# A Fourier layer's forward transform with the x table as the stationary operand, and its output turned by eight transposes

## The reference, cut to what matters

```
x_ft = rfft2(h)                                   # only 12 x 12 low modes of two corners are used
out_ft[:, :, :12, :12]  = einsum('bixy,ioxy->boxy', x_ft[:, :, :12, :12],  w1)
out_ft[:, :, -12:, :12] = einsum('bixy,ioxy->boxy', x_ft[:, :, -12:, :12], w2)
h = irfft2(out_ft) + conv_1x1(h)                  # 32 channels
h = layer_norm(h)                                 # over channels
h = gelu(h)                                       # not after the last layer
```

## Time and profile before

| | before |
|---|---|
| median of 3 runs | 7909.72 us (7907.23 to 7939.83) |
| profiled execution: its time, its span | 7906.27 us, 7904.4 us |
| PE busy / PEld busy | 86% / 58% |
| DVE, ACT, POOL busy | 62%, 64%, 54% |
| granted TensorE clock, mean | 0.922 of 2.4 GHz |
| DMA | 835 MB, 106 GB/s over the span |

### The profile page before, as it was taken

One profiled execution on the slowest core, in us unless ns is written; L12 is line 12 of the kernel. 1 busy time (PEld: TensorE's weight loads), 2 busy tenths in 40 slices (PEclk: granted clock), 3 DMA queues, 4 the chain that ended last, 5 costly groups with the idle time before them and its releaser, 6 DMA issues. The chain is left out here.

```text
span 7904.4 us, 141712 instructions
## 1 busy us (share of the span) xinstructions
PE 6788.2 (86%) x45682; PEld 4620.4 (58%) x45682; DVE 4865.3 (62%) x7585; ACT 5032.1 (64%) x8721; POOL 4262.9 (54%) x1540
## 2 busy tenths in 40 slices
PE   7888789999799999799998899999999477777777
PEld 4555577777677777577776544444444255444555
DVE  7888657777467777477776333333333566777774
ACT  7888567778477777477777477777777233333332
POOL 7888457777267777177776144444444433333330
PEclk9999899999899999899999999999999687788888
DMA  2222344444444444444444411111111322333330
GB/s 84 94 98 94 129 157 158 159 158 155 162 144 159 154 156 156 153 155 158 152 159 138 140 50 45 49 50 44 50 47 41 99 67 68 69 69 69 69 68 3
DMA packets 597044, 835.29 MB, mean 106 GB/s; under 512 B 451944, under 2 KB 493032, under 8 KB 531304
## 3 DMA queue, kind: packets, MB, share of 16 engines
q1 hardware_dynamic: 596968, 834.27, 33.9%
HBM read 477.54 MB, written 356.58 MB: 106 GB/s over the span
## 5 line engine op out<-in xcount | busy, mean ns | idle before, releaser
L859 POOL TENSOR_TENSOR sb_rstd<-sb_var,sb_minus_half 128x16 f32<-128x16 f32 x1280 | 3690.0, 2900 | 2440.3 <-DVE sb_var L591 1219.3
L598 DVE TENSOR_TENSOR sb_unit<-H,sb_rstd 128x512 f32<-128x512 f32 x768 | 527.3, 687 | 517.1 <-POOL sb_rstd L859 511.7
L555 ACT ACTIVATE sb_pix<-sb_unit 128x512 f32<-128x512 f32 x768 | 827.7, 1078 | 0.0
L505 PEld LDWEIGHTS M<-sb_table,sb_pix 128*128 128x128 f32 x6144 | 712.1, 194 | 144.3 <-ACT sb_pix L555 125.1
L478 PE MATMUL H<-sb_conv_block,sb_act_in 128*128 128x128 f32 x6144 | 777.7, 280 | 0.0
L551 ACT ACTIVATE sb_act_px<-sb_unit 128x512 f32<-128x512 f32 x768 | 485.9, 633 | 451.0 <-DVE sb_unit L604 450.9
L478 PEld LDWEIGHTS H<-sb_conv_block,sb_act_in 128*128 128x128 f32 x6144 | 724.3, 194 | 38.2 <-issue 23.9
L505 PE MATMUL M<-sb_table,sb_pix 128*128 128x52 f32 x6144 | 737.0, 279 | 0.0
L591 DVE TENSOR_REDUCE sb_var<-sb_square 128x16 f32<-128x528 f32 x768 | 502.5, 696 | 236.4 <-ACT sb_square L544 236.4
L822 DVE COPY sb_act_out<-TC 128x512 f32<-128x512 f32 x256 | 177.0, 691 | 644.3 <-PE TC L672 644.3
L1812 ACT ACTIVATE blk_silu<-bank 114x260 f32<-114x260 f32 x384 | 148.7, 387 | 638.4 <-PE bank L1598 635.8
(11 more groups left out here) (273 smaller groups left out, 13588.2 us busy)
## 6 DMA issues: line engine op xcount, KB each, us to landing
act_scratch<-sb_act_out SPq DMA_DIRECT2D x256, 1024.0 KB, 3.9
sb_act_in<-act_scratch SPq DMA_DIRECT2D x256, 1024.0 KB, 5.3
spectrum_in<-sb_f_sb SPq DMA_DIRECT2D x512, 78.0 KB, 1.8
sb_x_in<-spectrum_in SPq DMA_DIRECT2D x48, 832.0 KB, 4.3
spectrum_out<-sb_y_sb SPq DMA_DIRECT2D x48, 832.0 KB, 4.6
sb_z_in<-spectrum_out SPq DMA_DIRECT2D x512, 78.0 KB, 5.1
blk_rows_b<-scan_rows SPq DMA_DIRECT2D x128, 260.0 KB, 7.2
blk_rows_bb<-scan_rows SPq DMA_DIRECT2D x128, 260.0 KB, 8.2
```

Source lines behind the costliest of these rows:

```text
L505: mm = e.matmul(M[u][:, 52 * g:52 * g + 52], pix[1 - p][:, at:at + 128], const("f1"), start=True, stop=True)
L555: e.activation(dst, unit[k % 2][:, :].rearrange("p (x c) -> p c x", c=16), gelu).then_inc(pix_ready, 1)
L598: e.tensor_tensor(rows, H[k][:, :].rearrange("p (y c) -> p y c", c=C), rstd[k][:, :].unsqueeze(2).to_broadcast([128, 16, C]), ALU.mult).th ...
L859: e.tensor_tensor(rstd[j][:, :], var[j][:, :], minus_half[:, :], ALU.pow).then_inc(rstd_ready, 1)
```

## The change

forward_x no longer has the pixels as the stationary operand but the x table (52 columns), and the pixels of act_px as the moving one. It runs once for each chunk, right after to_channels, with two products of 256 columns: channels 0 to 15 go to partitions 0 to 51 of bank TP, channels 16 to 31 to partitions 64 to 115. So pix and its second gelu (or copy) are gone, and 16 products a pair become 8. Their output has the frequencies on the partitions; ACT copies TP to a new buffer `spread` after every two chunks (`gather`), and `turn` transposes spread by eight transposes into M[0] and M[1], from which ACT fills f1_sb as before (`frequencies`). forward_y writes M[1] in place of TP, and the copy to f2_sb moves from DVE to ACT (`spectrum`). In the first pass DVE's last step of the norm writes act_px itself, so that ACT's copy into act_px is gone too. The channels come in another order, which the tables "f2" and "combine" take up. The order of the three engines' programs is written anew.

```diff
@@ forward_x, the same in pe_first and pe_mid (before: 16 products of 52 columns)
-                e.wait_ge(pix_ready, g0)
-                for u in range(2):
-                    for g in range(8):
-                        at = 128 * (8 * u + g)
-                        mm = e.matmul(M[u][:, 52 * g:52 * g + 52], pix[1 - p][:, at:at + 128], const("f1"),
-                                      start=True, stop=True)
-                    mm.then_inc(f1_done, 1)
+                if k == 0:
+                    at_least(e, gathered, 2 * pr)
+                elif k == 2:
+                    e.wait_ge(gathered, 2 * pr + 1)
+                at = 16 * (k % 2)
+                src = act_px[k % 2][:, :].rearrange("p (y c) -> p y c", c=C)
+                for h in range(2):
+                    dst = TP[64 * h:64 * h + 52, :].rearrange("p (c y) -> p y c", y=32)[:, at:at + 16, :]
+                    mm = e.matmul(dst, const("f1"), src[:, :, 16 * h:16 * h + 16], start=True, stop=True,
+                                  skip_group_check=True)
+                mm.then_inc(fx_done, 1)
+            def turn(pr):
+                e.wait_ge(gathered, 2 * pr + 2)
+                for u in range(2):
+                    for b in range(4):
+                        at = 128 * (4 * u + b)
+                        mm = e.transpose(M[u][:, 128 * b:128 * b + 116], spread[0:116, at:at + 128],
+                                         const("ident")[0:116, 0:116])
+                    mm.then_inc(f1_done, 1)
@@ forward_y
-                    mm = e.matmul(TP[64 * i:64 * i + 48, 0:16 * T26], const("f2"), src, start=True, stop=True,
+                    mm = e.matmul(M[1][64 * i:64 * i + 48, 0:16 * T26], const("f2"), src, start=True, stop=True,
@@ act_mid
-                dst = pix[q][:, :].rearrange("p (c x) -> p c x", c=16)[:, :, 32 * k:32 * k + 32]
-                e.activation(dst, unit[k % 2][:, :].rearrange("p (x c) -> p c x", c=16), gelu).then_inc(pix_ready, 1)
+            def gather(half, pr):
+                e.wait_ge(fx_done, 4 * pr + 2 * half + 2)
+                at_least(e, f1_done, 2 * pr)
+                e.activation(spread[0:116, :].rearrange("p (c y) -> p c y", c=16)[:, :, 32 * half:32 * half + 32],
+                             TP[0:116, :].rearrange("p (c y) -> p c y", c=16), ACT.Copy).then_inc(gathered, 1)
+            def spectrum(q, pr, stored):
+                e.wait_ge(f2_done, pr + 1)
+                at_least(e, st_x[q], stored)
+                e.activation(f2_sb[q][:, :], M[1][0:112, 0:16 * T26], ACT.Copy).then_inc(f2_ready, 1)
@@ dve_first, normal
+                at_least(e, fx_done, c - 1)
+                e.tensor_tensor(act_px[k % 2][:, :].rearrange("p (y c) -> p y c", c=C), rows,
+                                shift_row[:, :].unsqueeze(1).to_broadcast([128, 16, C]), ALU.add).then_inc(px_ready, 1)
```

More of the change, by code:

```diff
@@ L519, in pe_mid @@
             if front:
+                conv(0)
                 inverse_x()
-            for j in range(4):
-                three = behind(g0, p, j, 3, front, back)
-                if front and j % 2 == 0:
-                    conv(j)
-                    conv(j + 1)
-                if three:
-                    to_channels(*three)
-                if front and j % 2 == 0:
-                    inverse_y(j)
-                    inverse_y(j + 1)
-                if back and j == 2:
-                    forward_x()
-                if back and j == 3:
-                    forward_y()
+                conv(1)
+            if back:
+                to_channels(g0 - 3, 1 - p, 1)
+                forward_x(1, it - 1)
+            if front:
+                inverse_y(0)
+                inverse_y(1)
+            if back:
+                to_channels(g0 - 2, 1 - p, 2)
+                forward_x(2, it - 1)
+            if front:
+                conv(2)
+                conv(3)
+            if back:
+                to_channels(g0 - 1, 1 - p, 3)
+                forward_x(3, it - 1)
+            if front:
+                inverse_y(2)
+                inverse_y(3)
+            if back:
+                turn(it - 1)
+            if front:
+                to_channels(g0, p, 0)
+                forward_x(0, it)
+            if back:
+                forward_y(it - 1)
         def act_mid(e, P, p, front, back):
@@ L568, in act_mid @@
                                  ACT.Copy).then_inc(v_ready, 1)
-            for j in range(4):
-                two, three = (behind(g0, p, j, lag, front, back) for lag in (2, 3))
-                if two and j == 0:
-                    gelus(*two)
-                if three:
-                    channels_out(*three)
-                if front and j % 2 == 0:
-                    squares(j)
-                    squares(j + 1)
-                if two and j > 0:
-                    gelus(*two)
-                if back and j == 2:
-                    for u in range(2):
-                        e.wait_ge(f1_done, 2 * it + u - 1)
-                        e.activation(f1_sb[:, 416 * u:416 * u + 416], M[u][:, 0:416], ACT.Copy).then_inc(f1_ready, 1)
+            if back:
+                gelus(g0 - 2, 2)
+                channels_out(g0 - 3, 1 - p, 1)
+                gather(0, it - 1)
+            if front:
+                squares(0)
+                squares(1)
+            if back:
+                channels_out(g0 - 2, 1 - p, 2)
+                gelus(g0 - 1, 3)
+                channels_out(g0 - 1, 1 - p, 3)
+                gather(1, it - 1)
+            if front:
+                squares(2)
+                squares(3)
+                gelus(g0, 0)
+            if back:
+                frequencies(0, it - 1)
+                frequencies(1, it - 1)
+            if front:
+                channels_out(g0, p, 0)
+            if back:
+                spectrum(1 - p, it - 1, 32 * (P if p else P - 1))
+            if front:
+                gelus(g0 + 1, 1)
         def dve_mid(e, P, p, front, back):
@@ L622, in dve_mid @@
                     normal(g0 + 1, 1)
-                if back and j == 3:
-                    spectrum()
         FC1 = (M[0], M[1], TP, H[3])
```

143 lines of the change are left out of this document (80 added, 63 removed).

## The result

The changed kernel takes 7949.1 us (median of 5 runs, 7936.39 to 7957.46) against 7909.72 (5 runs); the ratio is 1.0047, 95% interval 1.0027 to 1.0067. The time lies in the range for 8 in 10, but the forecast was 7812 and faster: the sign is wrong, and the likeliest case's own range, 7775 to 7860, doesn't hold it. The profiled execution's span went from 7904.4 to 7948.2, +43.8.

The account below looks back on a forecast made before the run. It took a 15.16 us loop through all four engines, plus clock drops, to bound the middle passes. 7906.3 - 85 (middle) - 13 (ends) + 0 (first pass) = 7808, 7812 as median; 8-in-10 range 7770 to 8040.

Parts of the forecast that it names:

- the likeliest case: Whole kernel: faster, 7775 to 7860 us, with a between 0.46 and 0.62 and the first pass between its ends; chance 0.58.
- a: Time of one chunk's new forward_x, two products of 256 columns: put at 0.50 us, near forward_y's rate.
- Rival 1: forward_x slow because of the output's stride or halves not overlapping: 8030 us, chance 0.14; if both, 8815 us, chance 0.10.
- half of 1.65 (...) comes back: +0.8: First pass: if the clock fell behind the image wait in every period, not every other, each would lose 0.8 us.
- -0.65 to +0.15: First pass: change per period in us, from shorter path to more clock drops; times 62, -40 to +9, taken as 0.
- the wait for the image stays near 2.8: First pass: PE's wait for the image load stays near 2.8 us, as PE's work behind forward_y is no longer.
- 13.90 + 2a: Middle passes: summed loop period, 14.90 us with a = 0.50, against 15.35; 0.45 a period, -85 us over three passes.
- rival 2: Gain eaten by small dues, product-group changes or the clock falling as before; only the ends left, about 7897 us; chance 0.12.
- the trace shows no such price there: Changing tiling mode costs PE nothing visible: to_channels to inverse_y takes 0.53 us, no more than the transposes alone.
- That the clock stays up: Middle passes: dense products replace forward_x's long stretch, so the clock mostly stays up, PEclk 0.99 to 1.00.
- The ends: Ends of passes: last gelu to f2_sb copy falls from 11.17 to 7.9 us; four ends, -13 us.
- The second loop: Middle passes: POOL's four powers, norm, sum and hand-over take 14.58 us; no change of PE and ACT alone goes below.

Follow-up runs that it names:

- experiment 2: Changed kernel with forward_x's output written to consecutive TP columns, without the stride (output order wrong, same work): 7948.89 us.
- experiment 1: Changed kernel with the first pass's image loads issued one pair earlier, ahead of the previous pair's stores: 7714.71 us, ratio 0.974 to the kernel before.
- experiment 9: Changed kernel with ACT's first-pass copy to f2_sb put ahead of the following lift's square: 7728.45 us, ratio 0.9772 to the kernel before.
- experiment 8: Changed kernel with first-pass forward_x of chunks 3 and 0, behind images_turned, cut to 32 columns a product instead of 256: 7853.32 us.
- experiment 10: Kernel before with two pairs of unread products in forward_x's new form added in the first pass, behind to_channels: 7969.36 us, ratio 1.0075.
- experiment 3: Changed kernel with middle-pass conv in one piece again, both chunks behind inverse_x: 7900.21 us, ratio 0.9967 to the kernel before.
- experiment 4: Changed kernel with the next pair's conv of chunk 0 right behind the turn in the middle passes: 7773.21 us, ratio 0.9821 to the kernel before.
- experiment 6: Kernel before with only the first pass's image load issued one pair earlier: 7809.39 us, ratio 0.9866.

## Why the prediction was wrong

- **What a is** was right: 0.50 was put, 0.47 and 0.57 were measured, and the stride, on which the forecast was said to stand or fall, costs nothing (experiment 2). Rival 1 is out.
- **The first pass: the step that failed.** "If it fell in every one, half of 1.65 (...) comes back: +0.8" took the low time's length, 3.3 us, from the kernel before. The wait came as forecast, and the path without a low time is indeed shorter (12.6 us, before 13.4; forecast -0.65). But the low time grew to 6.8 us and more. The period went from 13.65 us to 15.3 on the mean, +1.7 where -0.65 to +0.15 was put, and the pass became 95 us longer in place of -40 to +9. That "the wait for the image stays near 2.8" was a misreading besides: the 2.55 of the earlier trace rows is every other wait, the ones between are 1.3 to 1.5. Experiments 1 and 9 show that the wait is the cause of the low clock: without it, or with it at 0.4 to 1.1 us, the clock is at 1.00 and 221 to 234 us come back, the wait's own length among them. Why the low time is longer behind the change is open: thinning the products behind the wait shortens some (experiment 8), added ones come with some of 17 us (10), but neither run separates the products from the wait's place in time.
- **The middle passes: a sum of small dues.** 13.90 + 2a was put together from start-to-start times in the old neighbourhood. Each product group was taken as a constant; next to other groups four of them were 0.05 to 0.1 longer, and the stretch with conv cut in two 0.3 (experiment 3). So 14.90 became 15.37, and -85 us (with the clock's part) became -18: 971.2, 978.5 and 979.9 us from a pass's first store to its last became 966.7 each, and 3.9 each of that is the end. It is what rival 2 described, at 0.12. The rival's remark that "the trace shows no such price there" was a misreading: in the kernel before, the four transposes take 0.53 until inverse_y but 0.48 until conv, and conv's eight products take 1.89 behind inverse_x but 1.78 behind transposes. That the clock stays up was right (1.00). Only that part of the gain came: 14.90 was below the undisturbed 15.16, 15.37 is above it.
- **The ends** were right in size: 3.5 us each (forecast 3.3). Not forecast was the start of each middle pass, from the last store before it to its first: 161.6, 159.7 and 159.8 against 169.2, 168.3 and 167.0, 23 us together. Of the 7.6 us of the first stretch 4.9 lie ahead of the first to_channels, in the mixing, which the change leaves alone, and the first pair's start, at a granted clock of 0.89 against 0.87, and 2.7 behind it, at 0.91 against 0.74. So it goes with the clock; why the clock was higher there no run shows.
- **The second loop** at 14.58 was right but for 0.09: experiment 4 reaches 14.49, since the sum starts 0.08 before the last step of the norm ends, and the prediction counted that step to its end.
- **The range of the likeliest case** was added up wrongly: its own terms (a of 0.46 to 0.62, -40 to +9 in the first pass) give 7757 to 7866, not 7775 to 7860. The measured time lies outside either.
- All told: 95 (0 forecast), -18 (-85), -12 in the middle ends (-10; the first pass's own end is in the 95), -23 in the starts of the middle passes (0), +2 in the rest.

## What to carry to other kernels

Before costing an edit, look for a wait of the matmul engine that lies in a loop through a transfer's issue: there a copy moved by one instruction was worth 220 to 300 us of 7900, more than the whole new transform (186). Here the load issued one pair earlier took the wait away altogether (experiments 1 and 6). And when a path is summed from start-to-start times, add a due for each place where a group gets a new neighbour or is cut in two, and fill the wait that is left with work that needs nothing from it.

## What the runs showed of the hardware that was not expected

- The granted clock can stay at its lower level through 17 us in which PE had no gap (experiment 10), behind a wait of 1.96 us; waits of 0.4 to 1.1 us never brought it down between 60 and 740 us (experiment 9), and neither did those of 1.3 to 1.5 us in the kernel before, whose waits of 2.4 to 2.7 us each came with a low time of 3.4 us.
- In experiment 10 waits of 1.8 to 2.0 us were followed by no low time, by one of 3.4 us or by one of 17.
- fp32 products of 256 columns write PSUM at the same rate with neighbouring elements 128 bytes apart as with none apart: 420 ns a row either way (experiment 2).
- Conv's eight products took 1.78 us between transposes and 1.89 between inverse_x and transposes in the kernel before, and 1.09 + 1.00 cut in two with inverse_x between in the changed one.
